# Fuse phase of a four-layer graph network: ScalarE takes the finished sums out of PSUM, and the side work sits in other steps

## What is computed

```python
h = jnp.maximum(_layernorm(x, axis=-1), 0.0)
adj_d = _dilate(adj, mask)          # drops some neighbours of dense rows
def _sage(x, adj, Wr, Wx, b, mf):
    deg = jnp.clip(jnp.sum(adj, axis=-1, keepdims=True), 1.0, None)
    agg = jnp.einsum('bij,bjd->bid', adj, x) / deg
    out = agg @ Wr + x @ Wx + b
    nrm = jnp.maximum(jnp.linalg.norm(out, axis=-1, keepdims=True), NORM_EPS)
    return out / nrm * mf[..., None]
h1 = _bn(jax.nn.relu(_sage(h, adj_d, Wr1, Wx1, b1, mf)), g1, be1)
```

## Time and profile before

| | |
|---|---|
| median of 3 runs | 1270.97 us |
| the profiled execution, its own time | 1272.81 us |
| its span, first to last instruction | 1271.1 us |
| mean granted clock of TensorE | 0.957 of 2.4 GHz |
| busy: TensorE, its weight loads | 90%, 73% |
| busy: VectorE, ScalarE, GpSimd | 61%, 46%, 9% |
| fuse phase, first to last matmul of it | 322.4 to about 631 us |

### The profile page before, as it was taken

How to read it: one execution, slowest core, us unless ns; L and a number is a source line. 1 busy time by engine, 2 the same in 40 slices (tenths; PEclk the granted TensorE clock), 3 DMA queues, 4 the chain that set the end, 5 groups by cost and what they waited for, 6 DMA issues and landing times. The chain is left out here.

```text
span 1271.1 us, 26866 instructions
## 1 busy us (share of the span) xinstructions
PE 1149.8 (90%) x9713; PEld 930.8 (73%) x9713; DVE 769.3 (61%) x2819; ACT 589.4 (46%) x1533; POOL 114.6 (9%) x129
## 2 busy tenths in 40 slices
PE   4999889986798988989899999899998899996998
PEld 4999766754587777777699999699998555543554
DVE  5998587766556676666534545444545546546983
ACT  3888566777454455445303343413334433323441
POOL 3343000000000000000000000031323011010000
PEclk9999888875899999999999999999999999998999
DMA  8967011210465556662326664146666336633921
GB/s 329 336 266 276 24 31 28 36 19 15 167 265 201 191 207 250 248 233 117 130 110 259 254 244 183 51 166 229 269 238 243 133 133 265 250 147 146 406 61 50
DMA packets 105513, 228.92 MB, mean 180 GB/s; under 512 B 34528, under 2 KB 53152, under 8 KB 105376
## 3 DMA queue, kind: packets, MB, share of 16 engines
q1 hardware_dynamic: 104656, 227.07, 48.1%
q10 hardware_dynamic: 720, 0.07, 0.0%
HBM read 185.70 MB, written 37.75 MB: 176 GB/s over the span
## 5 line engine op out<-in xcount | busy, mean ns | idle before, releaser
L1459 PE MATMUL lay_acc<-lay_z,k_otheradj 128*128 128x128 f32 x1024 | 118.1, 277 | 0.0
L1459 PE MATMUL lay_acc<-lay_z,k_keepadj 128*128 128x128 f32 x1024 | 117.0, 275 | 0.0
L1459 PEld LDWEIGHTS lay_acc<-lay_z,k_otheradj 128*128 128x128 f32 x1024 | 116.9, 194 | 0.0
L1459 PEld LDWEIGHTS lay_acc<-lay_z,k_keepadj 128*128 128x128 f32 x1024 | 115.6, 192 | 0.0
L1507 ACT ACTIVATE lay_junk<-lay_o 128x128 bf16<-128x128 f32 x128 | 37.7, 296 | 125.2 <-DVEq L1596 125.0
L1573 DVE TENSOR_TENSOR lay_o<-lay_ring,k_vec 128x512 f32<-128x512 f32 x32 | 22.1, 692 | 108.2 <-PE lay_ring L1452 108.2
L1553 POOL TENSOR_TENSOR lay_bl<-k_vec,k_mask 128x256 f32<-128x256 f32 x32 | 21.2, 662 | 606.3 <-DVEq L1586 602.6
L333 PE MATMUL att_acc<-att_rhs,att_adjT 128*128 128x130 f32 x512 | 59.8, 280 | 13.5 <-POOLq L285 12.3
L333 PEld LDWEIGHTS att_acc<-att_rhs,att_adjT 128*128 128x128 f32 x512 | 59.2, 196 | 14.0 <-POOLq L285 12.4
L1190 ACT ACTIVATE fuse_dist<-fuse_prank,k_kb 128x512 f16<-128x512 f32 (+2 forms) x64 | 38.4, 599 | 60.7 <-PE fuse_prank L1080 59.3
L1141 PE MATMUL fuse_acc<-fuse_z,k_otheradj 128*128 128x129 f32 x512 | 63.6, 277 | 0.9 <-DVEq L1291 0.8
(11 more groups left out here) (294 smaller groups left out, 2563.0 us busy)
## 6 DMA issues: line engine op xcount, KB each, us to landing
k_keepadj<-in_adj_cols SPq DMA_DIRECT2D x28, 1024.0 KB, 9.2
k_keepadj<-keptT SPq DMA_DIRECT2D x12, 2048.0 KB, 10.8
k_otheradj<-keptT SPq DMA_DIRECT2D x12, 2048.0 KB, 10.9
att_adjT<-in_adj_cols SPq DMA_DIRECT2D x16, 1024.0 KB, 7.8
k_otheradj<-in_adj_cols SPq DMA_DIRECT2D x16, 1024.0 KB, 10.2
keptT<-k_keepadj SPq DMA_DIRECT2D x16, 1024.0 KB, 5.1
keptT<-k_otheradj SPq DMA_DIRECT2D x16, 1024.0 KB, 4.9
lay_rowf<-in_adj_rows SPq DMA_DIRECT2D x32, 512.0 KB, 14.6
```

The lines of the kernel that those rows point to most:

```text
L1459: mm = t.matmul(acc[i % 2][k][:, ib % HB, :], adjT[i % 2][:, jb, ib * P:(ib + 1) * P], zz[i % 2][:, jb, :], start=(jb == 0), stop=(jb == N ...
```

## The change

- `sums_out`: at step 0 ScalarE copies the three `acc` banks to a new SBUF tile `summed`, frees each (`acc_free`) and signals `summed_ready`. VectorE takes degrees (`degrees`, step 0) and sums (`outputs`, half at step 1, half at step 2) from `summed`.
- `squares` go to steps 2 and 3 and write their unused output over `summed`; `weights` to steps 3 and 4; `rectified` to 4 and 5; `batch_statistics` to 6 and 7.
- `turn_h` goes to steps 3 and 4, `turn_r` to steps 5 and 6; `norm_apply` to step 1.
- Row statistics are made two graphs ahead, at steps 4 and 5, root at step 6, scale at step 7; those of graph 1 before the first masks.
- `nrm` and the statistics' `stat` lie in the resident `maskok`, which nothing reads any more at this point; `junk` is gone.

```diff
@@ fuse_phase, buffers
-        junk = s.sb("junk", [P, NB, D], BF16)
-        nrm = s.sb("nrm", [P, 5, NB], F32)
+        summed = s.sb("summed", [P, NB, ZW], F32)
+        nrm = K["maskok"][:, 0:5 * NB].rearrange("p (k t) -> p k t", t=NB)
...
+        banks = ((0, 0, 3), (1, 3, 6), (2, 6, NB))
@@ misc_uses
-            if step in (3, 4) and b > 0:
-                uses.append(("turn_r", b - 1, step - 3))
-            if step in (5, 6) and b + 1 < B:
-                uses.append(("turn_h", b + 1, step - 5))
+            if step in (3, 4) and b + 1 < B:
+                uses.append(("turn_h", b + 1, step - 3))
+            if step in (5, 6) and b > 0:
+                uses.append(("turn_r", b - 1, step - 5))
@@ ScalarE
+                def sums_out(b):
+                    act.wait_ge(sums_ready, b + 1)
+                    for k, lo, hi in banks:
+                        a.activation(summed[:, lo:hi, :], accv[:, k, 0:hi - lo, 0:ZW], ACT.Copy)
+                        act.drain().then_inc(acc_free, 1)
+                    act.sem_inc(summed_ready, 1)
...
-                        a.activation(junk[:, ib, :], o[b % 2][:, ib, :], ACT.Square, accum_out=nrm[:, 0, ib:ib + 1])
+                        a.activation(summed[:, ib, 0:D], o[b % 2][:, ib, :], ACT.Square, accum_out=nrm[:, 0, ib:ib + 1])
...
                 for b in range(B + 1):
                     for st in range(NB):
+                        if b > 0 and st == 0:
+                            sums_out(b - 1)
                         if b + 1 < B:
                             distances(b + 1, st)
+                        if b > 0 and st == 5:
+                            rectified(b - 1, 1)
                         for use in misc_uses(b, st):
                             side_copy(*use)
-                        if b > 0 and st == 0:
-                            squares(b - 1, 0)
-                            squares(b - 1, 1)
-                        if b > 0 and st == 1:
+                        if b + 1 < B and st == 1:
+                            norm_apply(nc, act, x_tile(b + 1), h[:], w, b, h_ready)
+                        if b > 0 and st in (2, 3):
+                            squares(b - 1, st - 2)
+                        if b > 0 and st == 4:
                             rectified(b - 1, 0)
-                            rectified(b - 1, 1)
...
@@ VectorE
-                def outputs(b):
+                def degrees(b):
                     rdeg = K["rdeg"][:, b * NB:(b + 1) * NB]
-                    dve.wait_ge(sums_ready, b + 1)
...
+                    dve.wait_ge(summed_ready, b + 1)
+                    v.tensor_scalar(rdeg, summed[:, :, D], 1.0, None, ALU.max)
...
+                def outputs(b, half):
+                    for ib in range(half * HB, (half + 1) * HB):
                         out = o[b % 2][:, ib, :]
-                        v.scalar_tensor_tensor(out, acc_tile(ib)[:, 0:D], rdeg[:, ib:ib + 1], out, ALU.mult, ALU.add)
...
+                        v.scalar_tensor_tensor(out, summed[:, ib, 0:D], K["rdeg"][:, b * NB + ib:b * NB + ib + 1], out, ALU.mult, ALU.add)
+                    dve.drain().then_inc(out_ready, 1)
...
+                        if b > 0 and st == 0:
+                            degrees(b - 1)
...
+                        if b > 0 and st in (1, 2):
+                            outputs(b - 1, st - 1)
+                        if b > 0 and st in (3, 4):
+                            weights(b - 1, st - 3)
+                        if b + 2 < B and st in (4, 5):
+                            row_statistics(b + 2, st - 4)
+                        if b + 2 < B and st == 5:
+                            row_means()
+                        if b > 0 and st in (6, 7):
+                            batch_statistics(b - 1, st - 6)
+                        if b + 2 < B and st == 7:
+                            norm_scale(nc, dve, w, b + 1)
```

More of the change, by code:

```diff
@@ L78, in along_tiles, with norm_buffers @@
     return row.unsqueeze(1).to_broadcast([P, t, row.shape[1]])
-def norm_buffers(sb, sem, tag, NB):
-    return dict(stat=sb(f"{tag}_stat", [P, 3, NB], F32), part=sb(f"{tag}_part", [P, NB, 6], F32), pair=sb(f"{tag}_pair", [P, NB, 2], F32),
+def norm_buffers(sb, sem, tag, NB, stat=None):
+    return dict(stat=sb(f"{tag}_stat", [P, 3, NB], F32) if stat is None else stat, part=sb(f"{tag}_part", [P, NB, 6], F32), pair=sb(f"{tag}_pair", [P, NB, 2], F32),
                 mean_ready=sem(f"{tag}_mean_ready"), std_ready=sem(f"{tag}_std_ready"), scale_ready=sem(f"{tag}_scale_ready"),
@@ L1286, in outputs @@
                     dve.drain()
-                    for ib in range(NB):
+                def outputs(b, half):
+                    for ib in range(half * HB, (half + 1) * HB):
                         out = o[b % 2][:, ib, :]
-                        v.scalar_tensor_tensor(out, acc_tile(ib)[:, 0:D], rdeg[:, ib:ib + 1], out, ALU.mult, ALU.add)
-                        if ib in (2, 5, NB - 1):
-                            dve.drain().then_inc(acc_free, 1)
-                        if ib == HB - 1:
-                            dve.drain().then_inc(out_ready, 1)
-                    dve.sem_inc(out_ready, 1)
+                        v.scalar_tensor_tensor(out, summed[:, ib, 0:D], K["rdeg"][:, b * NB + ib:b * NB + ib + 1], out, ALU.mult, ALU.add)
+                    dve.drain().then_inc(out_ready, 1)
                 def weights(b, half):
@@ L1304, in weights, with batch_statistics, row_statistics, row_means @@
                         .then_inc(w_ready, 1)
-                def batch_statistics(b):
-                    for half in range(2):
-                        dve.wait_ge(rT_ready, b * 2 + half + 1)
-                        v.bn_stats(K["bnpart"][:, b * 2 + half, :], turned(T8, b)[:, half * HALF:(half + 1) * HALF])
-                def x_rows(b):
-                    return K["X"][:, b * NB:(b + 1) * NB, :]
+                def batch_statistics(b, half):
+                    dve.wait_ge(rT_ready, b * 2 + half + 1)
+                    v.bn_stats(K["bnpart"][:, b * 2 + half, :], turned(T8, b)[:, half * HALF:(half + 1) * HALF])
+                def row_statistics(b, half):
+                    for t in range(half * HB, (half + 1) * HB):
+                        v.bn_stats(w["part"][:, t, :], K["X"][:, b * NB + t, :])
+                def row_means():
+                    dve.drain()
+                    for t in range(NB):
+                        last = v.bn_aggr(w["pair"][:, t, :], w["part"][:, t, :])
+                    last.then_inc(w["mean_ready"], 1)
                 for nb in range(NB):
                     removals(0, nb)
+                    if nb in (2, 3):
+                        row_statistics(1, nb - 2)
+                    if nb == 4:
+                        row_means()
+                norm_scale(nc, dve, w, 0)
                 for b in range(B + 1):
@@ L1319, in _ @@
                             masked_rows(b, st)
-                        if b > 0 and st == 0:
-                            outputs(b - 1)
                         if b + 1 < B:
                             removals(b + 1, st)
+                        if b > 0 and st == 0:
+                            degrees(b - 1)
                         if b < B and st in (1, 2):
                             projected(b, st - 1)
-                        if b > 0 and st == 1:
-                            weights(b - 1, 0)
-                            weights(b - 1, 1)
-                        if b + 1 < B and st == 2:
-                            norm_mean(nc, dve, x_rows(b + 1), w)
-                        if b + 1 < B and st == 3:
-                            norm_scale(nc, dve, w, b)
-                        if b > 0 and st == 6:
-                            batch_statistics(b - 1)
+                        if b > 0 and st in (1, 2):
[5 more added lines that the diff above has]
+                        if b + 2 < B and st == 5:
+                            row_means()
+                        if b > 0 and st in (6, 7):
+                            batch_statistics(b - 1, st - 6)
+                        if b + 2 < B and st == 7:
+                            norm_scale(nc, dve, w, b + 1)
 def keep_busy(t, K, out, count):
```

13 lines of the change are left out of this document (6 added, 7 removed).

## The result

The changed kernel takes **1238.39 us** in the median of 4 runs (1236.61 to 1241.46), the kernel before in the same rounds 1271.62 us. The ratio is 0.9742, with a 95% interval of 0.972 to 0.9765: 33 us less. The forecast was 1239.0. The profiled execution took 1238.54 us; for it the forecast was 1240.8.

The account below looks back on a forecast made before the run. TensorE sets the pace but waits, mostly for VectorE's mask banks. Graphs 1 to 6 gain 31.5 us, graph 7 1.7, graph 0 0.6, less 0.3 and 1.6: 31.9, rounded to 32.0, from 1270.97 to 1239.0; range 1235 to 1248.

Parts of the forecast that it names:

- What a graph costs at full pace: Fuse phase: a graph with nothing late takes 32.3 us, so graphs 1 to 6 lose 5.3 us each.
- The rival that counted only visible idle time: Fuse phase: only TensorE's visible idle time is got back, 22.7 us in all, giving 1248; chance 0.06.
- The layout on VectorE: Graphs 1 to 6: spreading VectorE's lumps frees masks before TensorE needs them; all 5.3 us per graph should go.
- The tight place at step 4: VectorE's masks for TensorE's step 4 have the smallest slack, 0.6 us; elsewhere 1.2 or more.
- The copies on ScalarE: Three `sums_out` copies per graph, ahead of the first distance, take 1.7 us (1.2 to 2.1) of ScalarE's idle time.
- The 0.1 us per graph for the `misc` bank: Early in each graph, the copy of `z` ends just before TensorE asks for its bank: 0 to 0.2 us lost.
- The rule against the copy: Skill rule for one operation on PSUM: the copy is 1.7 us added per graph, 12 us if ScalarE set the pace.
- Turns and Relus: Moved `turn_h`, `norm_apply`, `turn_r` are ready before TensorE asks; in graph 0 this also removes a 0.68 us stall.
- First stretch, graph 7, end: Before graph 0's masks 0.3 us cost; graph 7 gains 1.7 (1.2 to 2.2); phase end costs 1.6 (1.1 to 2.1).
- The clock: TensorE's 1.2 GHz stretch at the phase's end may shift with the longer pause: 2.5 us either way, taken as 0.
- The transfers: DMA share rises to 0.69 per graph; as a rival, slowed loads make masks wait for chunks, 1277; slower 0.03.

Follow-up runs that it names:

- run 7: Changed kernel with the last graph's degrees and outputs read straight from PSUM and fillers 28, 4 and 8 in the last round: 1233.47 us.
- run 5: Changed kernel with VectorE, not ScalarE, making the three copies after its masks of row block 0: 1250.48 us.
- run 1: Changed kernel without ScalarE's copies; VectorE takes degrees and all eight outputs straight from PSUM at step 0: 1250.85 us.
- Run 9: Changed kernel with turn_r back in steps 3 and 4, turn_h in 5 and 6, squares, rectified and weights moved to suit, norm_apply in step 1: 1262.45 us.
- runs 6 and 7: The first is the changed kernel with more filler matmuls around the last round's half turns (34, 4, 8): 1237.32 us; the second is run 7.
- Runs 7 and 12: The second repeats run 7's program, beside the changed kernel on the same chip: 1233.05 us.

## Why the prediction was right

The mechanism came out as forecast: TensorE's waits for VectorE and ScalarE went, and each graph fell to its undisturbed length. That the median came within 0.6 us of the forecast is in part luck. In the traces the forecast's terms are 1.9 us short in sum (31.9 and 33.8), the stretch ahead of the phase gave another 0.5 that nothing in the change accounts for, and for the profiled execution the forecast of 1240.8 was 2.3 us too high.

- **What a graph costs at full pace.** The forecast was 32.3 us, from graph 0 less its own stall plus two half turns. It is 32.12: graph 0 without its stall takes 31.36, so a half turn costs 0.38 us and not the 0.45 taken. Over six graphs this term was 1.1 us short. The rival that counted only visible idle time (34 us per graph) is out: 5.5 us of length went for 3.4 us of idle time, so the length of an undisturbed graph was the right measure, not the idle column.
- **The layout on VectorE.** The forecast put the masks of row blocks 1 to 6 at 3.4, 7.8, 12.2, 14.9, 18.9 and 23.0 us. They start at 3.38, 7.59, 11.83, 14.57, 18.45 and 22.48. The forecast was slightly late from step 2 on, because it took 1.5 us for four outputs where they take 1.34 up to the next instruction; its 1.5 came from a row of eight with more drains in it (last section). The tight place at step 4 (slack 0.6) held with 0.8.
- **The copies on ScalarE.** 1.7 us were taken, 1.57 measured. The 0.1 us per graph for the `misc` bank, 0.6 in all, was not paid: `z` is copied at 2.13 us into the graph, as before.
- **The rule against the copy.** The Trainium skill ("VectorE: DVE Perf Modes", "Rules for kernel authors") would leave a single operation to read PSUM itself. At the end of the phase, where nothing covers the copy, run 7 agrees: without it the hand-over comes at 10.93 us in place of 12.70. Inside the graphs the copy by the idle ScalarE costs nothing, a copy by the busy VectorE 1.4 us per graph (run 5), and no copy 2.3 (run 1). That 2.3 is not the price of reading PSUM, though the prediction reads 0.35 us per output out of the earlier trace rows in that sense: it is the price of doing all eight outputs at step 0, which the copy makes unnecessary. Outputs straight from PSUM, spread over two steps, were not tried.
- **Turns and Relus.** Rows ready at 18.2 and 21.4 us were forecast, TensorE asking at 19.0 and 23.1. Measured: the Relus end at 18.45 and 21.62, the turns start at 18.88 and 22.92. The first has 0.4 us to spare. What the forecast undervalued is how much hangs on this edit: it said of the VectorE lumps that all 5.3 us would go by spreading them, and treated the exchange as a companion. Run 9 shows that the spreading gives only 2.4 of the 5.5 without it, since split outputs make the rows late for the old place of `turn_r`.
- **First stretch, graph 7, end.** +0.5 for +0.3, -2.2 for -1.7 (the upper bound), +1.8 for +1.6. The first stretch is 13.92 us in this trace, but 13.67 in run 7, whose program is the same there. Of the 1.8 us the first square accounts for 1.45 (3.43 behind the last sum, 1.98 before), and the second half turn, at 1.2 GHz, for the rest: from first turn to next phase 4.95 us, 4.48 before.
- **The clock.** The granted clock was 0.50 in the three stretches from 594 to 603 (and 0.98 before them, 0.81 behind); before, it was 0.75, 0.50 and 0.61 in the three from 630 to 639. The low stretch grew longer, but most of the added time was a pause. The fillers of the next phase took 5.28 us in both. The value taken, nothing, was right up to the half turn above; that the fall follows TensorE's pause is shown by runs 6 and 7, where filler in the pause kept the granted clock at 1.00 from 585 to 603 in both.
- **The transfers** were no bound: share 0.69, as worked out, and no wait on a chunk.

The edits are not additive. Taken out one at a time from the changed kernel, they cost per graph 2.3 us (copies and split outputs), 3.0 (exchange of turns) and 7.3 (statistics ahead), more than twice the 5.5 in all; alone, the copies give 0.6. It was not tried whether the exchange of turns would run alone in the kernel before.

## What to carry to other kernels

Price a reordering by laying each engine's work against the time at which the pacing engine asks for each bank or operand at full pace, and look for the smallest slack; an undisturbed stretch of the same kernel gives that pace better than the idle column does. Follow each producer chain to its end before moving one link, for a link that leaves later needs a consumer that asks later: half a rearrangement can be worth nothing. Where a move is free because other work hides it, treat the last round, where nothing does, by itself.

## What the runs showed of the hardware

- What a row of small VectorE instructions costs depends here on the drains in it and not on the memory it reads. Four outputs in a row take 1.14 us although each shows 0.35 as its duration: they start 0.26 us apart. Eight take 2.40 us from the copy and 2.37 straight from PSUM (run 7), each time with one drain between them, and 2.79 from PSUM with three (before, and run 1). That is about 0.2 us for each drain, an estimate from these rows. The mean duration of one, 347 ns before and after, shows none of it.
- The twelve fillers of the next phase: 0.44 us each at 1.2 GHz, 0.23 at 2.4 GHz. From the first of them to the layer's first matmul is 5.07 us at the low level (after) and 2.80 at the high one (run 7), although they compute nothing.
- Executions differ ahead of the fuse phase: the first mask of graph 0 came between 332.71 and 338.32 us in these traces, while the graphs of the changed kernel repeat to 0.01 us. The granted clock goes with it. Runs 7 and 12 are the same program; from 140 to 335 us, mostly `removal_phase`, they show 0.78 and 0.82 (windows view, columns as in the earlier trace rows):

```profile
140.00:335.00 195.00, 161.24 (x2215) 113.19 (x2213) 136.36 (x744) 126.61 (x229) 0.12 (x1) 0.78 0.18 40
...
140.00:335.00 195.00, 157.90 (x2235) 112.20 (x2235) 138.84 (x752) 128.85 (x234) 0.11 (x1) 0.82 0.19 43
```

  The first masks come at 338.17 and 333.07 us, and the whole executions took 1237.10 and 1232.05: the 5.1 us arise ahead of the phase. What decides it was not looked into. The profiled pair of before and after is alike in this (335.81 and 335.73), so its table compares like with like. Medians of runs a few microseconds apart say less here than the stretches of the trace.
